# The present key's term of the time mix's denominator made by GpSimd instead of ScalarE, with a new order of every engine's steps

## The reference

```python
# layer 0, time mix (width 512), per sequence
k = exp(minimum(xk @ tm_Wk, 60)); v = xv @ tm_Wv; r = xr @ tm_Wr; kv = k * v
# scan over the tokens: sk, skv are the decayed sums of the tokens before
wk, wkv = first * k + sk, first * kv + skv
rwkv = sigmoid(r) * (wkv / (wk + 1e-8))
x = x + rwkv @ tm_Wo
# channel mix: x = x + sigmoid(xr @ cm_Wr) + silu(xk @ cm_Wk) @ cm_Wv
# then a soft decision tree of depth 8 (gates -> leaf probabilities -> leaf values)
# layer 1: causal attention, 16 heads of width 8, rotary; then 16 experts, the two best per token
```

## Time and profile before

| | us |
|---|---|
| median of 3 runs | 1709.79 (1707.97 to 1712.36) |
| the profiled execution, its own time | 1714.23 |
| its span, first to last instruction | 1711.8 |
| mean granted TensorE clock, share of full | 0.959 |
| PE busy | 1570.9 (92%) |
| DVE busy | 1418.7 (83%) |
| ACT busy | 1025.3 (60%) |
| POOL busy | 913.5 (53%) |

### The profile page before, as it was taken

How to read it: one execution, slowest core, us unless ns; L and a number is a source line. 1 busy time by engine, 2 the same in 40 slices (tenths; PEclk the granted TensorE clock), 3 DMA queues, 4 the chain that set the end, 5 groups by cost and what they waited for, 6 DMA issues and landing times.

```text
span 1711.8 us, 33755 instructions
## 1 busy us (share of the span) xinstructions
PE 1570.9 (92%) x12127; PEld 1094.8 (64%) x12205; DVE 1418.7 (83%) x3018; ACT 1025.3 (60%) x2110; POOL 913.5 (53%) x1233
## 2 busy tenths in 40 slices
...
GB/s 112 1 6 56 7 57 8 34 31 18 53 8 58 14 56 8 47 24 26 46 8 63 9 57 8 55 17 34 37 13 58 9 57 2 63 2 52 13 14 7
DMA packets 66969, 53.35 MB, mean 31 GB/s; under 512 B 8370, under 2 KB 65522, under 8 KB 66802
## 3 DMA queue, kind: packets, MB, share of 16 engines
...
## 4 chain that ended last, share of the span: by engine, by line
PE 77%; DVE 11%; ACT 3%; issue 3%; SPq 2%; POOL 2%; DMA 1%; another core or an unknown queue 0%; DVEq 0%; ACTq 0%; POOLq 0%
PE bank L962 73%; PE bank L958 4%; SPq L318 2%; DVE rall L788 2%; DVE rall L786 1%; DVE mixed L693 1%; DVE stats L684 1%; DVE rall L784 1%; ACT prob L525 1%; DVE inner L693 1%; DVE wkb L732 1%; DMA kh<-part 1%; DVE xc L814 1%; DVE mv L689 1%; ACT gT L525 0%
## 5 line engine op out<-in xcount | busy, mean ns | idle before, releaser
L525 ACT ACTIVATE prob<-bank 128x512 f32<-128x512 f32 x640 | 355.7, 597 | 131.7 <-PE bank L962 130.0
L962 PEld LDWEIGHTS bank<-wexpT,prob 128*128 128x128 f32 x2048 | 264.7, 193 | 29.2 <-issue 24.9
L962 PE MATMUL bank<-kh,qh 72*128 72x512 bf16 (+3 forms) x1024 | 250.6, 306 | 23.2 <-DVE rall L786 11.2
L962 PE MATMUL bank<-wexpT,prob 128*128 128x128 f32 x2048 | 265.6, 276 | 2.8 <-DVE prob L863 0.3
L461 POOL TENSOR_TENSOR prob<-xdT,spread 128x512 f32<-128x512 f32 x128 | 162.7, 1271 | 192.6 <-ACT spread L525 163.8
L962 PE MATMUL bank<-qh,kh 75*128 75x512 bf16 (+3 forms) x1024 | 242.7, 303 | 6.1 <-ACT prob L525 5.7
L732 DVE RECIPROCAL wkb<-wkb 128x512 f32<-128x512 f32 x64 | 214.0, 3344 | 0.0
L962 PE MATMUL bank<-maskb,identb 128*128 128x128 bf16 x1024 | 192.9, 223 | 0.0
L962 PE MATMUL bank<-maskTb,identb 128*128 128x128 bf16 x1024 | 190.3, 220 | 0.0
L786 DVE TENSOR_REDUCE rall<-bank 128x4 f32<-128x512 f32 x256 | 175.1, 684 | 16.4 <-PE bank L962 15.4
L788 DVE TENSOR_REDUCE rall<-bank 128x1 f32<-128x512 f32 x256 | 174.7, 682 | 16.3 <-PE bank L962 16.1
...
## 6 DMA issues: line engine op xcount, KB each, us to landing
...
```

Source lines behind the costliest of these rows:

```text
L525: raised(act.activation(dst, src, func, **kw), signal)
L962: return pe.matmul(out_, w, x, start=start, stop=stop, **kw)
```

## The change

`k_first` leaves ACT's list and becomes a POOL step, a `tensor_scalar` (times `first[:, c]`, plus the epsilon as an immediate number), ahead of `wk`. It waits for the same things. DVE's `yc` gets a wait for `xc`. All four lists are written anew; SP's list is as before. The diff, the lists cut to the parts that the text speaks of:

```diff
 pool
-        1:root1 4:gate_prob 4:gates 4:gate_rest 4:gate_lo 2:cmr_sig 2:cmr_sum 4:u1 4:u3 2:root3 ... 4:u7 4:u9 1:wk0
-        4:u11 4:u13 4:u15 3:max_left_hi1 3:max_left_mid1 1:wk1 1:r_sig0 1:r_sig1 1:gated0 1:rwkv0 1:gated1 1:r_sig2 1:wk2 1:rwkv1 2:root_rms 1:wk3
-        1:gated2 1:r_sig3 2:rope_sum0 1:gated3 2:rest0 1:rwkv2 2:part_lo0 2:rope_sum1 1:rwkv3 2:rest1 2:part_lo1 0:root0 1:root2
+        1:k_first3 1:gated2 2:rope_sum0 1:wk3 2:rest0 1:r_sig3 1:rwkv2 1:gated3 2:part_lo0 2:rope_sum1 1:rwkv3 2:rest1 2:part_lo1 0:root0 1:root2
+        ... 3:gate_prob 3:gates 1:cmr_sig 3:gate_rest 3:gate_lo 1:cmr_sum ...
+        3:u7 0:k_first0 3:u9 0:wk0 3:u11 3:u13 0:r_sig0 3:u15 0:k_first1 0:wk1 2:max_left_hi1 0:gated0
+        2:max_left_mid1 0:r_sig1 0:rwkv0 0:k_first2 1:root_rms 0:gated1 0:r_sig2 0:rwkv1 0:wk2
 act (lags as written; the new list is also rotated, so that its lags are one less for the same work)
-        3:pvT_out0 3:exp32 2:part_hi1 3:exp33 3:exp34 2:part_mid1
+        3:pvT_out0 3:exp32 3:exp33 2:part_hi1 2:part_mid1 3:exp34
 dve
-        ... 1:ksum1 1:kvsum1 1:clamp2 1:inverse0 4:yd 1:wkv1 1:inverse1 1:ksum2 2:yb 2:moments4 1:kv2 1:clamp3 1:kvsum2 1:kv3 1:wkv2 ...
+        ... 0:ksum1 0:kvsum1 0:inverse0 1:yb 3:yd 1:moments4 0:wkv1 0:inverse1 0:kv2 1:clamp3 1:kvsum2 1:ksum2 1:wkv2 2:rope_mul0 1:kv3 ...
-        3:route_probs 3:others 2:rowmax11 3:largest1 2:rowmax12
+        3:route_probs 3:others 3:largest1 2:rowmax11 2:rowmax12
 pe
-        2:row8 2:row9 1:cmk2 2:row10 2:row11 3:xdT 1:cmk3 3:centroids 1:cmr 2:row12 3:shared 1:cmv0
+        2:row8 1:cmk2 2:row9 2:row10 3:xdT 1:cmk3 3:centroids 3:shared 2:row11 1:cmr 2:row12 1:cmv0
-        2:row14 2:row15 1:cmv3 3:gT 2:row16 2:row17 3:gb0 3:biases
+        2:row14 2:row15 3:gT 1:cmv3 2:row16 3:gb0 3:biases 2:row17
-        3:score18 3:score19 3:weigh4 3:weigh5 3:weigh6 2:xcT 1:r3 3:score20 3:score21 2:rope0 2:rope1
+        2:score12 0:k3 1:xcT 2:score13 0:v3 2:score14 2:score15 1:rope0 2:score16 2:score17 1:rope1 2:score18 2:score19

+            def key_first(b, c):
+                if b == 0 and c == 0:
+                    pool.wait_ge(setup["decay1"], 2)
+                until(pool, b, "k_exp", c + 1)
+                reached(pool, "rwkv", C * b + c - 1)
+                raised(pool.tensor_scalar(wkb[:, c % 2, :], kk[:, c % 2, :], first[:, c:c + 1], K_EPS, ALU.mult, ALU.add), "k_first")
+
             def weight_sum(b, c):
+                until(pool, b, "k_first", c + 1)
                 until(pool, b, "k_sum", c + 1)
-                until(pool, b, "k_first", c + 1)
                 raised(pool.tensor_tensor(wkb[:, c % 2, :], wkb[:, c % 2, :], ksum[:, c % 2, 0:T], ALU.add), "wk")
...
-            def key_first(b, c):
-                move(b, wkb[:, c % 2, :], kk[:, c % 2, :], "k_exp", "k_first", c + 1, freed=[("rwkv", C * b + c - 1)],
-                     scale=first[:, c:c + 1], bias=keps[:, 0:1])
...
             def add_attention(b):
                 until(dve, b, "proj_ps")
+                until(dve, b, "xc")
```

More of the change, by code:

```diff
@@ L65 @@
[L65 to L68, removed]
@@ L69 @@
-        1:weights 1:mix_before3 1:mix_before4 4:norm7 1:cmk_tanh0 1:cmk_tanh1 3:norm6 1:cmk_tanh2 3:xdT_out 1:cmk_tanh3 2:norm4 3:route_exp 2:values
-        1:cmr_tanh 3:gate_hi 3:gate_mid 3:gT_out 0:norm1 3:spread1 0:mix_before0 3:spread3 0:mix_before1 0:mix_before2 2:max_hi0 3:spread5 1:norm3
-        2:max_mid0 2:max_lo0 2:maxT_out0 3:spread7
+        2:norm_rms 3:exp11 3:exp12 3:exp13 2:xcT_out 3:exp14 3:exp15 1:k_exp3 3:exp16 3:exp17 3:exp18 3:exp19 3:exp20 3:exp21 3:exp22 3:exp23
+        2:part_hi0 3:exp24 3:exp25 1:r_tanh3 3:exp26 3:exp27 3:exp28 2:part_mid0 3:exp29 3:exp30 3:exp31 3:pvT_out0 3:exp32 3:exp33 2:part_hi1
@@ L72 @@
+        2:max_hi1 1:leafT_out0 2:exp2 2:exp3 1:leafT_out1 2:max_mid1 2:exp4 2:exp5 0:k_exp2 2:max_lo1 2:exp6 2:exp7 2:exp8 2:exp9 2:maxT_out1
+        0:r_tanh2 2:exp10
     """,
     dve="""
-        3:rowmax25 1:mix2 3:rowmax26 3:rowmax27 1:clamp0 4:u8 3:rowmax28 3:rowmax29 1:kv0 1:kvsum0 3:rowmax30 4:u10 2:tree0 3:rowmax31 1:ksum0
-        2:tree1 3:rowmax32 1:wkv0 3:rowmax33 3:rowmax34 4:u12 1:clamp1 2:tree2 3:rowmax35 2:tree3 3:rowmax36 3:rowmax37 4:u14 2:tree4 3:rowmax38
-        2:tree5 3:rowmax39 1:kv1 2:tree6 3:max_join1 2:tree7 1:ksum1 1:kvsum1 1:clamp2 1:inverse0 4:yd 1:wkv1 1:inverse1 1:ksum2 2:yb 2:moments4
@@ L77 @@
[L77 to L80, removed]
@@ L81 @@
-        1:moments3 2:rowmax19 2:rowmax20 3:u4 2:max_join0 2:rowmax21 2:rowmax22 0:mix0 2:rowmax23 2:rowmax24 3:u6 0:mix1
+        1:clamp3 1:kvsum2 1:ksum2 1:wkv2 2:rope_mul0 1:kv3 1:kvsum3 2:rope_mul1 1:ksum3 1:inverse2 1:wkv3 2:rope_mul2 2:rope_mul3 1:inverse3
+        1:weights 0:moments0 3:attend0 4:moments7 1:x2 1:moments2 2:rowmax0 2:rowmax1 3:attend1 2:rowmax2 2:rowmax3 2:rowmax4 2:rowmax5 1:mix3 3:yc
+        1:mix4 3:moments6 2:rowmax6 2:rowmax7 1:silu0 2:rowmax8 1:silu1 0:moments1 2:rowmax9 1:silu2 2:rowmax10 3:route_logits 1:silu3 3:largest0
@@ L82 @@
+        1:tree7 0:clamp2 2:max_join1 0:ksum1 0:kvsum1 0:inverse0 1:yb 3:yd 1:moments4 0:wkv1 0:inverse1 0:kv2
     """,
     pe="""
-        4:expert4 2:xbT 3:row25 3:maxT0 4:gb7 4:expert5 3:row26 3:row27 4:gb8 1:k0 4:expert6 3:row28 3:row29 4:gb9 1:v0 2:gates0 2:gates1 3:row30
-        4:gb10 4:expert7 3:row31 3:row32 4:gb11 1:r0 4:expert8 1:v1 3:row33 3:row34 4:gb12 1:k1 4:expert9 3:row35 3:row36 4:gb13 4:expert10 3:row37
-        4:gb14 4:expert11 3:row38 3:row39 4:gb15 4:expert12 4:expert13 1:r1 4:expert14 4:expert15 3:score0 3:score1 1:k2 3:score2 3:score3 2:leafT0
@@ L87 @@
[L87 to L94, removed]
+        3:score26 1:weights 3:score27 2:rope3 3:score28 3:score29 3:weigh8 3:weigh9 3:weigh10 3:score30 3:score31 3:weigh11 3:score32 3:score33
```

28 lines of the change are left out of this document (22 added, 6 removed).

## The result

The changed kernel takes 1728.45 us, median of 3 runs (1726.03 to 1729.66), against 1709.79: 1.0104 times as long, 95% interval 1.0082 to 1.0125. The change costs 18.7 us where 3.5 were forecast, and the time lies 3.5 us above the range. The profiled execution took 1728.45 us, its span 1726.3.

The account below looks back on a forecast made before the run. Turns were taken as bound by PE with DVE close behind, the start by chains through DVE. Terms 5.7 + 1.4 - 3.6 = +3.5 us on 1709.79 gave 1713.3 us; the 8-in-10 range was 1697 to 1725.

Parts of the forecast that it names:

- The gates: largest1 ahead of rowmax11, gT ahead of cmv3: PE's 0.29 us wait before biases should go, -0.24 us a turn.
- cmk2: With row9 now behind cmk2, PE stands still for row9's 0.34 us while waiting for silu0: +0.34 us a turn.
- row0 behind exp33: exp33 ahead of part_hi1 delays the keys' transfers and row0: +0.38 us in 15 sequences, +5.7 us, the dearest term.
- The sign that I gave for it: Row0's first load on PE would wait near 0.9 us for kh<-part.
- The instruction: k_first's 64 activations move from ACT to POOL's idle time: 0.62 us each, bounds 0.61 to 1.27, price 0 on the path.
- 12 us upstream: k_first3 was said to lie some 12 us ahead of rwkv3 on POOL, beside waits for DVE.
- The start: yb and moments4 ahead of wkv1 and inverse1 bring xcT, hence the first row0, earlier: -3.6 us, bounds -5 and 0.
- the end: The kernel's end has no time mix; priced at 0, give or take 1 us.
- my 15 and 14 times: Multipliers in the sum: 0.38 us for 15 sequences at row0, and +0.10 us in each of 14 turns for cmk2 and gates.
- The rival of the port: New POOL instructions hold two-input DVE instructions at the shared SBUF port: +0.9 us a turn, 13 us, 1726; chance 0.04.
- The rival of xcT: PE waits at xcT for moments4 and what follows: 0.4 to 0.6 us a turn, priced 7 us, 1720; chance 0.2.

Follow-up runs that it names:

- experiment 13: Kernel before with only two steps moved: largest1 ahead of rowmax11 on DVE, gT ahead of cmv3 on TensorE; 1712.93 us, ratio 1.0014.
- experiment 5: Changed kernel with one step shrunk to one column: k_first3 (1727.55 us), all four k_first (1725.72) or gated2 (1726.04).
- experiment 6: Changed kernel with part_hi1 ahead of exp33 again on ScalarE, nothing else; 1724.07 us, ratio 1.0079.
- experiment 7: Changed kernel with gated2 moved behind rope_sum0 on POOL, nothing left out; 1730.09 us, ratio 1.0119.
- experiment 1: Kernel before in its old order, only k_first moved to POOL, directly ahead of wk; 1767.85 us, ratio 1.0329.
- experiment 2: Kernel before, old order, k_first on POOL ahead of wk but shrunk to one column from the second sequence on; 1766.64 us, ratio 1.0331.

## Why the prediction was wrong, step by step

- **The gates, -0.24 us a turn: wrong in sign**, +0.29. I credited the wait that goes and didn't follow `rowmax11` to the rows behind it. This is shown in the kernel before (experiment 13), and the changed kernel has the same delays up to `row16`; undoing the two moves there was not run. It is one of the two largest parts of the turn's growth, with `rwkv3`'s 0.31.
- **cmk2, +0.34: 0.** The wait is there (0.68 us) and costs nothing. Together with the line above: the forecast took each wait of TensorE in the rows for lost time; these two show that what counted was whether DVE's next row maximum came later.
- **row0 behind exp33, +0.38: there, 0.32, but not where I put it.** With `rwkv3` in time (experiment 5) `row0` waits 0.3 us for the transfers, and ScalarE runs `exp33` and `part_hi1` without a pause between them. In the changed kernel `read_out0` is itself 0.31 us late and covers that. The two are alternatives, not terms. The sign that I gave for it, a wait near 0.9 us of the first load, read 0.5:
```profile
PEld bank L966 <- DMA kh<-part: 0.5, 1, 0.5
```
  No run has `rwkv3` in time and `part_hi1` first together, so what the turn would then be is open.
- **The instruction, price 0 on the path: nearly right for its length**, 0.05 us a turn; but the queue that ends with `rwkv3` was on the path, and TensorE's 0.31 us there stood at nothing in my sum. The duration was 0.70, not 0.62 alone (bounds 0.61 to 1.27), and 1.72 beside a scan, over the upper bound. "12 us upstream" (it was 13) was no distance: POOL has no pause in between.
- **What the sum left out in the turn:** +0.25 us beside the parts above (0.13 in the rows, 0.12 in the scores). Of the rows' part 0.07 goes with the instruction's length (experiment 5). The other 0.18 no run brought back, and its cause stays open; up to 0.05 of it can lie in the division by equal work. Forecast and measurement of a turn differ by 0.33 = 0.53 (gates) - 0.34 (cmk2) - 0.07 (the tie) + 0.25 - 0.03 (`read_out0` to `row0`), within rounding.
- **The start, -3.6: -0.4.** `xcT` did come 4.3 us earlier, much as worked out (0.6 + 3.3), but `read_out0` only 0.2. Changed kernel, TensorE, then DVE:
```profile
125.57 1.12 PE L962 MATMUL bank<-ident,xch 128*128 128x128 f32 x4 [2.87 <-ACT xch L551]
...
145.32 5.53 PE L966 MATMUL bank<-wo,inner 128*128 128x128 f32 x32 [11.40 <-POOL inner L416]
```
```profile
132.65 2.31 DVE L722 TENSOR_TENSOR_SCAN ksum<-decay,kk 128x512 f32<-128x512 f32 x1
```
  The same collision stands here, and POOL's list ahead of `rwkv3` runs without a pause from 130.94 to it. I moved one input earlier and took the output to follow.
- **Irregular turns, 3.2 us, and the end, 1.2: not foreseen.** The first are waits for the keys' transfers, most of them in one turn of one execution; with `part_hi1` 0.5 us earlier (experiment 6) all turns of its execution are equal. Whether each execution of the changed kernel has such a turn isn't shown. Of the end I know only the size.
- **Sum by the spans:** 3.5 forecast + 4.3 (13 x 0.33) less 0.9 that my 15 and 14 times held over 13 + 3.2 (start) + 3.2 + 1.2 = 14.5.
- **The rival of the port, chance 0.04:** the mechanism was present in every changed order. I gave it so little on reading that scans stayed within 1158 to 1221 ns, which are the key scans alone. "Only POOL lengthened in this loop" was a misreading, and the trace of before showed the contrary outside the scans. DVE, then POOL, in its start:
```profile
69.17 1.28 DVE L895 TENSOR_SCALAR w_rope<-prob 128x64 f32<-128x64 f32 x1
...
70.50 1.31 DVE L902 CAST brow_part<-prob 48x128 bf16<-48x128 f32 x1
```
```profile
69.08 1.30 POOL L386 TENSOR_TENSOR x<-x,g 128x512 f32<-128x512 f32 x1
70.45 1.27 POOL L390 TENSOR_TENSOR x<-x,b 128x512 f32<-128x512 f32 x1
```
  Such a `TENSOR_SCALAR` takes 0.21 us. In the turn, too, `wkv3` at 511.50 took 1.40 instead of some 0.7. Which of the two engines was lengthened went with the order of arrival, and that differs by hundredths of a microsecond. As the price of this change it stays unproven, but for 0.07 us a turn: taking a collision of the scores away (experiments 5 and 7) gave 0.05 or nothing back. In the old order (experiments 1 and 2) a lengthened instruction is the first difference and accounts for 1.1 of the 3.8 us; for the other 2.7 it is argued from the wait for `xch`.
- **The rival of xcT, chance 0.2:** no such wait in the changed kernel's usual turns; it came in experiment 1, by way of `root_rms`.
